# Self-attention in a decoder layer: value products of 130 columns, output in five pieces, one 16-bit copy of the probabilities on VectorE

## Time and profile before

| | |
|---|---|
| median of three runs | 2322.6 us |
| the profiled execution | 2315.09 us, its span 2313.3 us |
| mean granted clock of TensorE | 0.992 |
| busy: TensorE | 2178.3 us, 94% of the span |
| busy: ScalarE | 1612.0 us, 70% |
| busy: VectorE | 1552.2 us, 67% |
| busy: GpSimd | 1542.5 us, 67% |
| L597 differences on GpSimd | 448, 986.7 us busy |
| L909 reductions on VectorE | 1024, 679.8 us busy |
| L836 and L828 exponentials | 512 each, 571.0 and 568.1 us busy |
| L695, L697, L710 value products | 4096 each, 320.0, 318.1 and 208.0 us busy |

### The profile page before, as it was taken

One profiled execution on the slowest core, in us unless ns is written; L12 is line 12 of the kernel. 1 busy time (PEld: TensorE's weight loads), 2 busy tenths in 40 slices (PEclk: granted clock), 3 DMA queues, 4 the chain that ended last, 5 costly groups with the idle time before them and its releaser, 6 DMA issues. The chain is left out here.

```text
span 2313.3 us, 62611 instructions
## 1 busy us (share of the span) xinstructions
PE 2178.3 (94%) x22392; PEld 1254.6 (54%) x22392; DVE 1552.2 (67%) x2573; ACT 1612.0 (70%) x1831; POOL 1542.5 (67%) x1008
## 2 busy tenths in 40 slices
PE   6988999999997989899989899999999978998999
PEld 3544666666665455444445456666666644554444
DVE  5897777777776666753368977777777767667532
ACT  3556999999998556731145579999999975566210
POOL 5644988989988577721246368998989976867210
PEclk9999999999999999999999999999999999999999
DMA  4220000000001301103112100000000022021000
GB/s 105 56 49 3 4 7 9 9 9 9 9 0 28 100 6 39 46 12 81 46 51 56 42 1 10 0 9 9 9 9 9 9 61 64 2 47 38 19 23 33
DMA packets 102348, 65.23 MB, mean 28 GB/s; under 512 B 75346, under 2 KB 75346, under 8 KB 102226
## 3 DMA queue, kind: packets, MB, share of 16 engines
q1 hardware_dynamic: 102226, 63.57, 12.5%
HBM read 46.69 MB, written 8.39 MB: 24 GB/s over the span
## 5 line engine op out<-in xcount | busy, mean ns | idle before, releaser
L597 POOL TENSOR_TENSOR qkn<-wide 128x1024 f16<-128x1024 f32 x448 | 986.7, 2234 | 136.5 <-PE bank L710 120.7
L909 DVE TENSOR_REDUCE sq<-bank 128x1 f32<-128x512 f32 x1024 | 679.8, 688 | 246.8 <-PE bank L666 244.1
L836 ACT ACTIVATE wide<-bank,shift 128x1024 f32<-128x1024 f32 x512 | 571.0, 1115 | 37.3 <-DVE qkn L923 30.7
L828 ACT ACTIVATE wide<-bank,shift 128x1024 f16<-128x1024 f32 x512 | 568.1, 1110 | 9.9 <-PE bank L682 9.9
L681 PE MATMUL bank<-q_hh,ko 128*128 (+1 forms) x1024 | 388.9, 380 | 18.5 <-ACT wide L836 13.6
L666 PE MATMUL bank<-ko,q_hh 128*128 (+1 forms) x1024 | 387.7, 380 | 10.7 <-DVE sq L909 7.1
L682 PE MATMUL bank<-q_lm,k_h 65*128 (+1 forms) x1024 | 389.0, 380 | 0.0
L695 PEld LDWEIGHTS bank<-v_hl,wide 128*128 128x128 f16 x4096 | 287.6, 98 | 63.4 <-issue 5.7
L695 PE MATMUL bank<-v_hl,wide 128*128 (+1 forms) x4096 | 320.0, 192 | 0.1
L697 PE MATMUL bank<-v_hl,wide 128*128 (+1 forms) x4096 | 318.1, 193 | 0.0
L697 PEld LDWEIGHTS bank<-v_hl,wide 128*128 128x128 f16 x4096 | 267.5, 96 | 58.7
(11 more groups left out here) (228 smaller groups left out, 4213.2 us busy)
## 6 DMA issues: line engine op xcount, KB each, us to landing
wide<-in_x SPq DMA_DIRECT2D x32, 256.0 KB, 2.7
q_lm<-in_x SPq DMA_DIRECT2D x32, 256.0 KB, 3.2
ko<-in_L_ffn_W SPq DMA_DIRECT2D x32, 256.0 KB, 4.1
q_hh<-q_hh SPq DMA_DIRECT2D x32, 128.0 KB, 2.6
ko<-k_h SPq DMA_DIRECT2D x32, 128.0 KB, 2.8
out<-bo_b SPq DMA_DIRECT2D x16, 256.0 KB, 2.0
out<-xbo_b SPq DMA_DIRECT2D x16, 256.0 KB, 2.0
q_lm<-sq SPq DMA_DIRECT2D x248, 0.2 KB, 4.9
```

The source lines that it names most:

```text
L597: pool.tensor_tensor(probs_l[:, p % 2, :], probs[:, p % 2, :], probs_h[:, p % 4, :], ALU.subtract).then_inc(pl_pool, 1)
L828: act.activation(probs_h[:, p % 4, :], SB[p % 2][:, :], ACT.Exp, bias=shift[:, 0:1]).then_inc(ph_ready, 1)
L836: act.activation(probs[:, p % 2, :], SB[p % 2][:, :], ACT.Exp, bias=shift[:, 0:1]).then_inc(p_ready, 1)
L909: dve.tensor_reduce(pm[:, s, k:k + 1], MB[k % 2], AX_X, ALU.max).then_inc(mx_free, 1)
```

## The change

In TensorE's high products, the two products with the same probabilities become one of 130 columns for three of the four query tiles (`WIDE` = 3); its high and low columns go to different columns of `OB`. 4 x 130 columns do not fit into a bank of 512, so the fourth tile keeps its two products. The unused column of `v_hl` is now set to one as well, since it is read.

VectorE's output has therefore two sums to add: reciprocal, multiplication of the high columns (four tiles in one instruction), and one scalar_tensor_tensor for each of the three wide tiles, which multiplies its low columns and adds them. These five pieces (`output(u, s, step)`) stand behind reductions 4 to 8, one each.

For pair 6 (`CAST`), ScalarE no longer makes the 16-bit copy. VectorE makes it from the 32-bit one (`probs_high`), as a sum with a column of one 16-bit zero that is broadcast over 1024 elements (`null`). It stands behind reduction 11. `probs_low` moves from behind reduction 10 to behind reduction 9. TensorE's high products and GpSimd's difference of pair 6 wait for the new semaphore `ph_dve`.

```diff
@@ pool
-  pool.memset(v_hl ... [:, :, DH:DH + 1], 1.0)
+  pool.memset(v_hl ... [:, :, DH:DH + 2], 1.0)
   ...
       pool.wait_ge(p_ready, G + p + 1)
+      if p == CAST:
+          pool.wait_ge(ph_dve, U0 + u + 1)
+          pool.nop(nofuse=True)
@@ values_high(u, p, ob)
-  pe.wait_ge(ph_ready, (U0 + u) * PAIRS + p + 1)
+  if p == CAST:
+      pe.wait_ge(ph_dve, U0 + u + 1)
+  else:
+      pe.wait_ge(ph_ready, (U0 + u) * (PAIRS - 1) + (p if p < CAST else p - 1) + 1)
   ...
-      o0 = t * (DH + 1)
-      pe.matmul(ob[:, o0:o0 + DH + 1], rows, vf[:, bass.ds(v0, DH + 1)], ...)
-      pe.matmul(ob[:, o0:o0 + DH], rows, vf[:, bass.ds(v0 + DH + 2, DH)], ...)
+      o0 = t * VW
+      wide = VW if t < WIDE else DH + 1
+      pe.matmul(ob[:, o0:o0 + wide], rows, vf[:, bass.ds(v0, wide)], ...)
+      if t >= WIDE:
+          pe.matmul(ob[:, o0:o0 + DH], rows, vf[:, bass.ds(v0 + DH + 2, DH)], ...)
@@ act
-  act.activation(probs_h[:, p % 4, :], SB[p % 2][:, :], ACT.Exp, bias=shift[:, 0:1]).then_inc(ph_ready, 1)
+  if p != CAST:
+      act.activation(probs_h[:, p % 4, :], SB[p % 2][:, :], ACT.Exp, bias=shift[:, 0:1])\
+          .then_inc(ph_ready, 1)
@@ dve
+  def probs_high(u):
+      p = CAST
+      dve.wait_ge(p_ready, (U0 + u) * PAIRS + p + 1)
+      dve.tensor_tensor(probs_h[:, p % 4, :], probs[:, p % 2, :], null[:, :].broadcast_to([P, 2 * CT]),
+                        ALU.add).then_inc(ph_dve, 1)
   ...
+  # output(u, s, step): step 0 reciprocal, step 1 multiplication of all high columns, and then
+  t = step - 2
+  if t == 0:
+      dve.wait_ge(o_high, U0 + u + 1)
+  low = dve.scalar_tensor_tensor(
+      out=o_u[:, t, :], in0=OB[s][:, t * VW + DH + 2:(t + 1) * VW], scalar=rden[:, t:t + 1],
+      in1=o_u[:, t, :], op0=ALU.mult, op1=ALU.add)
@@ unit(u, s, first, maxed), for k in range(16)
-      if k == 4 and not first:
-          output(u - 1, 1 - s)
-      if k == (6 if first else 2 * (DVE_PAIR + 1)):
+      if 4 <= k < 4 + 2 + WIDE and not first:
+          output(u - 1, 1 - s, k - 4)
+      if k == (6 if first else 2 * DVE_PAIR + 1):
           probs_low(u)
+      if k == (9 if first else 2 * CAST - 1):
+          probs_high(u)
@@ before the first unit
   dve.tensor_copy(eye16[:, :], ident[:, :]).then_inc(e_eye, 1)
+  dve.memset(null[:, :], 0.0).then_inc(e_null, 1)
+  dve.wait_ge(e_null, b + 1)
@@ after the last unit
-  output(UNITS - 1, 1)
+  for step in range(2 + WIDE):
+      output(UNITS - 1, 1, step)
```

More of the change, by code:

```diff
@@ L227, in decoder_layer @@
         ph_ready = sem("ph_ready")
+        ph_dve = sem("ph_dve")
+        e_null = sem("e_null")
         p_ready = sem("p_ready")
@@ L236, in decoder_layer @@
         o_rec = sem("o_rec")
+        o_high = sem("o_high")
         o_free = sem("o_free")
@@ L471, in decoder_layer @@
                     pm, nm_, rden = (sq[:, n:n + k] for n, k in ((256, 32), (288, TPC), (296, TPC)))
+                    null = sq[:, 300:301].bitcast(F16)[:, 0:1]
                     pm = pm.rearrange("p (s n) -> p s n", s=2)
@@ L496, in decoder_layer @@
                     AHEAD = 6
+                    CAST = 6
+                    WIDE = TPC - 1
                     vf = v_hl
@@ L584, in _ @@
                         pool.nop(nofuse=True)
-                        pool.memset(v_hl[:, :].rearrange("p (k e) -> p k e", e=VW)[:, :, DH:DH + 1], 1.0)\
+                        pool.memset(v_hl[:, :].rearrange("p (k e) -> p k e", e=VW)[:, :, DH:DH + 2], 1.0)\
                             .then_inc(a_ones, 1)
@@ L693, in values_high @@
                                     rows = probs_h[:, p % 4, half * CT + t * P:half * CT + t * P + P]
-                                    o0 = t * (DH + 1)
-                                    pe.matmul(ob[:, o0:o0 + DH + 1], rows, vf[:, bass.ds(v0, DH + 1)],
+                                    o0 = t * VW
+                                    wide = VW if t < WIDE else DH + 1
+                                    pe.matmul(ob[:, o0:o0 + wide], rows, vf[:, bass.ds(v0, wide)],
                                               start=(p == 0 and half == 0 and t == 0), stop=False, skip_group_check=True)
-                                    pe.matmul(ob[:, o0:o0 + DH], rows, vf[:, bass.ds(v0 + DH + 2, DH)],
-                                              start=False, stop=False, skip_group_check=True)
+                                    if t >= WIDE:
+                                        pe.matmul(ob[:, o0:o0 + DH], rows, vf[:, bass.ds(v0 + DH + 2, DH)],
+                                                  start=False, stop=False, skip_group_check=True)
                         def values_low(u, p, ob):
@@ L928, in o_out, with output @@
                             return of[:, bass.ds(first, TPC * P)].rearrange("p (t d) -> p t d", d=P)[:, :, 0:DH]
-                        def output(u, s):
-                            o4 = OB[s][:, 0:TPC * (DH + 1)].rearrange("p (t e) -> p t e", e=DH + 1)
+                        def output(u, s, step):
+                            skip = s * (TPC * VW - CT)
+                            four = pairs[3][:, s * CT - skip:s * CT - skip + TPC * VW].rearrange("p (t e) -> p t e", e=VW)
                             r4 = rden[:, :].rearrange("p (t a) -> p t a", a=1)
[L934 to L938, removed]
+                            o_u = o_out(u)
+                            if step == 0:
+                                dve.wait_ge(lo_done, (U0 + u + 1) * PAIRS + 2)
+                                dve.reciprocal(r4, four[:, :, skip + DH:skip + DH + 1]).then_inc(o_rec, 1)
+                            elif step == 1:
+                                dve.wait_ge(o_rec, U0 + u + 1)
+                                dve.tensor_tensor(o_u, four[:, :, skip:skip + DH], r4.broadcast_to([P, TPC, DH]), ALU.mult)\
+                                    .then_inc(o_high, 1)
+                            else:
+                                t = step - 2
[4 more added lines that the diff above has]
+                                    in1=o_u[:, t, :], op0=ALU.mult, op1=ALU.add)
+                                if t == WIDE - 1:
+                                    low.then_inc(o_free, 1)
                         def split_both(pieces):
```

## The result

| | before | changed |
|---|---|---|
| median | 2321.52 us (4 runs, 2315.88 to 2323.47) | 2363.63 us (4 runs, 2362.0 to 2365.64) |
| ratio of the times | | 1.0186, 95% interval 1.0166 to 1.0206 |
| profiled execution, its span | 2315.09, 2313.3 | 2365.64, 2363.9 |
| mean granted clock | 0.992 | 0.985 |

The forecast was 2359, or 36.8 us over the kernel before; measured are 42.1.

What follows compares the result with a forecast made beforehand. TensorE was taken as the bound, GpSimd close behind. Units of 17.61 against 17.12 us gave +27.4, first units +2.4, last units +7: +36.8, so 2359 us on the median's scale; own range 2338 to 2372, 8-in-10 range 2278 to 2374.

Steps and rivals of the forecast that it cites:

- late maximum product at step 7: TensorE, step of key-block pair 7: its maximum product waits for reductions queued behind the held sum, 1.28 us per unit.
- late starts of step 6 gone: TensorE, step of key-block pair 6: too long by 0.51 or 0.33 us; pair 4's earlier difference on VectorE removes this.
- late start behind the output gone: TensorE: a maximum product 0.19 us late because VectorE made the output between two maxima; the five pieces remove it.
- GpSimd's own circle: GpSimd's time per unit, from one pair 5 difference to the next, with pair 6 waiting for the sum: 17.4 us.
- turn of the loop: TensorE: extra time where the loop, which holds two units, turns: 0.46 us, counted as 0.23 per unit.
- tail of a batch: Last unit of each batch: pair 5's difference starts 1.2 us later, output ends at 754.9 instead of 751.4: +3.5 us.
- part 4: VectorE's sum for pair 6 waits for GpSimd's pair 5 difference, ending 1.09 us after it; TensorE loses 1.28 per unit.
- Parts 1 to 3: Savings per unit: 130-column products 0.14 us, output in five pieces 0.19, pair 4's difference one maximum earlier 0.51 or 0.33.
- (a): Rival at step 7: the broadcast column does not hold sum and GpSimd apart; unit 16.3 us, time 2286, faster; chance 0.24.
- (b): Rival: the sum gets in before GpSimd's pair 5 difference, so GpSimd waits and not TensorE; about 2341 us; chance 0.08.
- (c): Rival: the stall is there, but savings are larger or other late starts vanish in it; 2318 to 2327 us; chance 0.06.
- (d): Rival: wide products or output pieces dearer than their rows, on top of the forecast; 2370 to 2415 us; chance 0.06.

Runs made afterwards that it cites:

- run 2: Changed kernel, with VectorE's 16-bit copy of pair 6 made as a maximum over an axis of length 1 instead of the sum: 2289.4 us.
- run 5: Changed kernel without the sum (ScalarE copies pair 6), and with VectorE's difference of pair 4 back behind reduction 10: 2308.6 us.
- run 4: Changed kernel with narrow value products (65 and 64 columns) and the output in two pieces, sum kept: 2370.9 us.
- run 1: Changed kernel without VectorE's sum: ScalarE makes the 16-bit copy of pair 6 again, the other parts stay: 2280.6 us.
- run 3: Changed kernel with the sum behind reduction 12 instead of 11: 2347.7 us.
- run 7: Changed kernel, with GpSimd making the difference for only the first 512 of 1024 columns of its seven pairs: 2289.4 us.
- run 8: Changed kernel, with VectorE's copy of pair 6 as a tensor_scalar multiplication by 1 instead of the sum: 2329.2 us.

## Why the prediction was right

| term, us per unit | predicted | measured |
|---|---|---|
| late maximum product at step 7 | 1.28 | 1.31 and 1.22 (changed), 0.07 (run 2) |
| late starts of step 6 gone | 0.51 and 0.33 | steps of 2.00; 0.48 by run 5 |
| late start behind the output gone | 0.19 | steps of 2.01 |
| wide products | 0.14 | 0.12 (run 4), 0.06 at run 1's pace |
| GpSimd's own circle | 17.4 | 17.45 (run 3), 17.44 (changed, every second unit) |
| turn of the loop, mean | 0.23 | about 0.35 |
| whole unit | 17.61 | 17.74 |
| tail of a batch, us | +3.5 | +4.1 |
| first units of a batch, us | +1.2 | +0.8 |

- *The hold (part 4).* As forecast: the sum is issued at once, waits for GpSimd's whole instruction and ends 1.08 behind it, and what is paid for is the reduction queued behind it. Runs 2 and 7 show that it is the hold, run 1 that the rest of the change is no loss. The Trainium skill, "SBUF — State Buffer", section "Who interferes with whom", states the rule for two SBUF inputs; the traces agree (2.45 against 1.22), here with a broadcast column as the second. The same section names tensor_scalar among the instructions that can contend and tensor_reduce as one that never does: runs 8 (1.92 us) and 2 (1.22 us) agree.
- *Parts 1 to 3.* Gains, as forecast. The product of 130 columns lies on the line between 65 and 512: ten products take 0.46. The 81 ns of the Trainium skill, "TensorE: Matmul & The Clock Gate", section "Back-to-back issue gap", are not seen; three wide products and one narrow one take 0.20 (710.74 to 710.94 in the trace), 57 ns for a wide one.
- *The sum.* The path and the hold were right; some terms were sized too small. Mid units gave 0.64 instead of 0.49 each. The missing 0.15 is two things (less 0.05, as eight steps of 2.006 are 16.05, not 16.10). The first: the turn of the loop costs 0.35 per unit and not 0.23. The 0.46 per turn that I took from the kernel before was right for it: its two steps around the turn took 2.19 and 2.32 (from 674.46 and 676.64), 0.45 over two of 2.03, and run 1 has 0.48. In the changed kernel it is 0.69, the added part in the step with the late product (0.36 instead of 0.16); why is open. The second: in every second unit TensorE's own time, 16.05 + 1.31 = 17.36, is under GpSimd's circle, and the unit takes 17.44; two of its steps wait for GpSimd's 2.09. I had compared the two circles in the mean only (17.61 and 17.4), but the units with the turn and those without have different bounds.
- *The tail.* It was 0.6 short, as pair 5's difference in the last unit started 1.9 later and not 1.2 (764.41 - 727.40 against 741.68 - 706.56).
- *The whole.* Both batches from the first difference on GpSimd to the end of the last output grew by 22.1 and 22.5 us, 44.6 together, where 36.8 was forecast for the whole; the medians moved by 42.1. The forecast of 2359 against 2363.6 is thus a little closer than its terms: it stands on a median of 2322.6 for the kernel before, which is 2321.5 with the fourth run. The two profiled executions differ by 50.6; the other 6.0 lie in code that is the same in both, where TensorE was granted its 1.2 GHz level for longer (mean clock 0.985 against 0.992). That the clock is the reason for the 6.0 is not tested.
- *Rivals.* (a) is refuted by the rows of L938. (b) did not happen: pair 5 on GpSimd starts 0.76 before the sum is issued, much as worked out (0.66). (c) is out by size. (d) is out by the 0.46 of ten products and by run 4, where narrow ones are slower; the 64-column pieces took 0.28, not 0.22, with no effect, as they stand beside free time (the three in a row at the end of a batch took 0.67, as forecast).

## What to carry to other kernels

Before work is moved to an engine that looks idle, ask what it shares with the others, and what is queued behind the new instruction there: VectorE had 28% free and the copy needed 1.2 us in 17, but as a sum it could run only when GpSimd paused, and the reductions behind it fed TensorE through two banks. The 1.2 us that the sum was held cost VectorE nothing that it lacked; they cost the work queued behind it, and so TensorE and GpSimd. If a copy must go there, choose a form that is not held (run 2: a reduction over one element, 74 us better than the sum), but look first whether the engine that it relieves was the bound at all: leaving the copy with ScalarE was best.

## What the runs showed of the hardware

- A reduction over an axis of length 1 is a conversion of 128 x 1024 elements from 32 to 16 bits in 1.22 us that GpSimd never delayed in run 2 (64 of 64 between 1210 and 1222 ns, all begun beside a difference on GpSimd), although the tensor_scalar form, 0.68 alone, took 1.92 beside it in run 8.
- A held VectorE instruction ends as if its own work began about 0.13 before GpSimd's recorded end: 1.22 of work ends 1.08 or 1.09 after it, in the kernel before, the changed one and run 7 alike, and 0.68 of work (run 8) 0.55 after it.
- A tensor_tensor with one input in PSUM and a broadcast column on the chip (L964) took 416 to 426 ns, beside GpSimd or not; the sum, with two inputs on the chip, was held every time.
- The turn of the loop over two units costs TensorE 0.45 us in the kernel before and 0.69 in the changed one, in the two steps around it: 3.59 - 2.01 - 1.22 = 0.36 and 2.34 - 2.01 = 0.33 in the changed kernel.
